# Two-layer conditioned attention, second layer: shifted-score matmuls put singly between key and query matmuls

## The reference

```
xn = layer_norm(x, norm_w, norm_b)
q = (xn @ q_w + q_b).reshape(Bx, Tx, H, -1)
k = (xn @ k_w + k_b).reshape(Bx, Tx, H, -1)
att = softmax(einsum('bnhl,bmhl->bnmh', q, k) + (1.0 - mask) * -1000000.0, axis=2)
v = ((xn @ v_w + v_b) * src_mask[:, :, None]).reshape(Bx, Tx, H, -1)
y = einsum('bnmh,bmhl->bnhl', att, v).reshape(Bx, Tx, Dx)
h = layer_norm(y, sb_norm_w, sb_norm_b) * (1.0 + scale) + shift
return x + silu(h) @ out_w + out_b
```

## Time and profile before

| what | value |
|---|---|
| median of 3 runs | 2480.9 us (2477.12 to 2482.09) |
| profiled execution | 2484.31 us, its span 2482.5 us |
| TensorE matmul records | 2359.0 us, 95% of the span |
| TensorE weight loads | 2125.6 us, 86% |
| VectorE, ScalarE, GpSimd | 63%, 33%, 24% |
| mean granted TensorE clock | 0.967 of full speed |
| layer 2, one body without disturbance | 41.2 us |

### The profile page before, as it was taken

How to read it: one execution, slowest core, us unless ns; L and a number is a source line. 1 busy time by engine, 2 the same in 40 slices (tenths; PEclk the granted TensorE clock), 3 DMA queues, 4 the chain that set the end, 5 groups by cost and what they waited for, 6 DMA issues and landing times.

```text
span 2482.5 us, 43830 instructions
## 1 busy us (share of the span) xinstructions
PE 2359.0 (95%) x15670; PEld 2125.6 (86%) x15670; DVE 1557.4 (63%) x3441; ACT 823.2 (33%) x1893; POOL 601.7 (24%) x847
## 2 busy tenths in 40 slices
PE   7999999999999999968999999999999999999998
PEld 5888888888888888857989898998889898989897
DVE  4677777777777777654465655556565656555654
ACT  2233333333333333332333333333323333333332
POOL 0333333333333333232121212122221212121210
PEclk9999999999999999978999989999989999989997
DMA  6100000000000010014444434353524343433432
GB/s 238 72 34 35 36 35 34 34 34 34 34 34 34 34 35 34 25 47 95 105 96 111 94 91 114 86 120 86 120 73 115 90 117 89 117 83 100 105 93 54
DMA packets 90933, 187.14 MB, mean 75 GB/s; under 512 B 18708, under 2 KB 29394, under 8 KB 90904
## 3 DMA queue, kind: packets, MB, share of 16 engines
q1 hardware_dynamic: 88856, 186.23, 28.3%
q10 hardware_dynamic: 2048, 0.53, 0.1%
HBM read 51.81 MB, written 33.69 MB: 34 GB/s over the span
## 4 chain that ended last, share of the span: by engine, by line
PE 47%; DVE 5%; issue 2%; POOL 1%; DMA 0%; ACT 0%; DVEq 0%; POOLq 0%; SPq 0%
PE bank L1423 7%; PE bank L439 5%; PE bank L441 5%; PE bank L440 5%; PE bank L430 5%; PE bank L431 5%; PE bank L1413 4%; PE bank L432 4%; PE bank L1439 4%; DVE h_lo L1207 2%; DVE z L1176 1%; DVE stats_y L1181 1%; POOL ve_y L1073 1%; POOL rstd_y L1075 1%; PE bank L1372 1%
## 5 line engine op out<-in xcount | busy, mean ns | idle before, releaser
L439 PE MATMUL bank<-xT_hi,w_hi 128*128 128x256 f32 x1536 | 446.4, 291 | 2.6 <-DVE xT_lo L1145 1.4
L440 PE MATMUL bank<-xT_lo,w_hi 128*128 128x256 f32 x1536 | 448.1, 292 | 0.0
L441 PE MATMUL bank<-xT_hi,w_lo 128*128 128x256 f32 x1536 | 445.0, 290 | 0.0
L1154 DVE SCALAR_TENSOR_TENSOR parts<-bank,qk_bias,parts 128x256 fp32r<-128x256 f32 x256 | 112.1, 479 | 432.9 <-ACT parts L1284 432.9
L1423 PEld LDWEIGHTS bank<-v,prob 128*128 128x128 f32 x2048 | 317.6, 195 | 12.7
L430 PE MATMUL bank<-w_hi,xT_hi 128*128 128x512 f32 x768 | 317.0, 413 | 0.0
L432 PE MATMUL bank<-w_lo,xT_hi 128*128 128x512 f32 x768 | 314.6, 410 | 0.0
L431 PE MATMUL bank<-w_hi,xT_lo 128*128 128x512 f32 x768 | 314.4, 409 | 0.0
L439 PEld LDWEIGHTS bank<-xT_hi,w_hi 128*128 128x128 f32 x1536 | 293.2, 191 | 4.8 <-DVE xT_lo L1145 1.8
L440 PEld LDWEIGHTS bank<-xT_lo,w_hi 128*128 128x128 f32 x1536 | 293.3, 191 | 1.9
L1423 PE MATMUL bank<-v,prob 128*128 128x33 f32 x2048 | 293.3, 251 | 0.0
(11 more groups left out here) (163 smaller groups left out, 4232.9 us busy)
## 6 DMA issues: line engine op xcount, KB each, us to landing
stack<-parts SPq DMA_DIRECT2D x768, 128.0 KB
xr<-in_x SPq DMA_DIRECT2D x32, 512.0 KB, 3.5
x_between_layers<-x SPq DMA_DIRECT2D x64, 256.0 KB, 2.0
xr<-x_between_layers SPq DMA_DIRECT2D x32, 512.0 KB, 3.6
out<-y_out SPq DMA_DIRECT2D x64, 256.0 KB, 2.0
w_emb<-in_L_cond_W_emb SPq DMA_DIRECT2D x4, 1024.0 KB, 9.9
w_emb<-in_L_cond_emb_w SPq DMA_DIRECT2D x4, 1024.0 KB, 4.8
raw<-in_L_cond_Wq SPq DMA_DIRECT2D x1, 1024.0 KB, 5.5
```

Of the source, the lines that this page charges most:

```text
L439: yield nc.tensor.matmul(dst, w_hi[:, m, c, fs], a_hi[:, c], start=(first and c == 0), stop=False)
L440: yield nc.tensor.matmul(dst, w_hi[:, m, c, fs], a_lo[:, c], start=False, stop=False)
L441: yield nc.tensor.matmul(dst, w_lo[:, m, c, fs], a_hi[:, c], start=False, stop=(c == C - 1))
L1154: nc.vector.scalar_tensor_tensor(parts[:, LO[n], c].rearrange("p b t -> p (b t)"), ps[QK_BANKS[n][c // 2]][:, at:at + PAIR * P], qk_bias[: ...
```

## The change

`weight_scores` becomes a generator that gives a step after every matmul. In the bodies with a previous pair, its 16 matmuls for the first sequence are put singly behind the first 16 of the 24 matmuls of key blocks 2 and 3, and those for the second sequence behind the first 16 of the 24 of query blocks 0 and 1. Behind the loop the two runs of 16 stay as they are. The transpose of the maxima keeps its place behind the 16th key matmul, and the two waits on `top` keep theirs ahead of key blocks 0 and 2.

```diff
--- before.py
+++ after.py
@@ -1412,7 +1412,9 @@
                 for a in range(HC):
                     last = nc.tensor.matmul(ps[W_BANKS[j]][:, a * P:(a + 1) * P], stack[0:K_SHIFTED, 1, a, j, b, :],
                                             stack[0:K_SHIFTED, 0, a, j, b, :], start=True, stop=True)
-                last.then_inc(s["w_ps"], 1)
+                    if a == HC - 1:
+                        last.then_inc(s["w_ps"], 1)
+                    yield
 
         def mixed(prev, b):
 
@@ -1453,18 +1455,19 @@
 
         def body(i, first, more, last):
             pe.wait_ge(s["xT_lo"], seq(PAIR, i, PAIR))
-            for f in range(C):
-                if not first and f % 2 == 0:
-
-                    pe.wait_ge(s["top"], seq(PAIR * C, i - 1, C + f // 2 + 1))
-                keys = projected(i, 1, (f,))
-                if not first and f == 1:
-                    run(islice(keys, 4))
-                    shift_row(i - 1, 1)
-                run(keys)
-                if not first and f % 2:
-                    weight_scores(i - 1, f // 2)
-            run(projected(i, 0, (0, 1)))
+            if not first:
+
+                pe.wait_ge(s["top"], seq(PAIR * C, i - 1, C + 1))
+            keys = projected(i, 1, (0, 1))
+            run(islice(keys, 16))
+            if not first:
+                shift_row(i - 1, 1)
+            run(keys)
+            if not first:
+
+                pe.wait_ge(s["top"], seq(PAIR * C, i - 1, C + 2))
+            woven(projected(i, 1, (2, 3)), () if first else weight_scores(i - 1, 0))
+            woven(projected(i, 0, (0, 1)), () if first else weight_scores(i - 1, 1))
             if first:
                 run(projected(i, 0, (2, 3)))
             else:
@@ -1497,7 +1500,7 @@
         bodies(pe, NP, body)
         shift_row(NP - 1, 1)
         for b in range(PAIR):
-            weight_scores(NP - 1, b)
+            run(weight_scores(NP - 1, b))
         for b in range(PAIR):
             run(mixed(NP - 1, b))
         for b in range(PAIR):
```

## The result

The changed kernel takes 2486.0 us (median of 10 runs, 2483.3 to 2490.8); the kernel before, run beside it, 2478.2 us (10 runs, 2475.1 to 2486.4). The ratio is 1.0031, its 95% interval 1.0019 to 1.0043: 7.8 us slower, and clear of no change. The forecast was 2472.5 us, faster. The executions that were profiled lie above these medians: 2484.31 us for the kernel before, and for the changed kernel the slowest of its ten.

A forecast was written before the change was run, and what follows sets the result against it. TensorE was taken as the bound, its matmul records covering 95% of the span. From the profiled 2484.3 us, 3.7 direct and 4.7 clock gave 2475.9, or 2472.5 on the median; range 2456 to 2487.

The forecast's parts named there:

- What a score costs between long matmuls: Step pricing a single shifted score among key or query matmuls: 0.108 us, against 0.112 in a burst.
- fixed part: Constant of about −0.004 us per group of short matmuls, fitted as 0.1122 n − 0.004 for a group of n.
- stated ends: Limits for a single score's price: 0.102 us (9.9 us less in all) and 0.1195 us (7.4 us more).
- direct term: TensorE time saved on 992 woven scores: (0.112 − 0.108) × 992 = 3.7 us less, 0.12 us a body.
- single transpose: Transpose of the maxima, one short matmul among keys, priced at 0.10 us and taken as the low end.
- "switching" rival: Each woven score costs a full key's 0.1195 us: 7.4 us more plus a clock fall, 2488.3 to 2494.6; chance 0.14.
- The clock term: TensorE's granted clock falling to 1.2 GHz in five loop bodies, just after pair-end waits; each fall costs 4.7 to 6.3 us.
- one fall fewer: Chosen as likeliest: four clock falls in the loop instead of five, 4.7 us less.
- The two waits: TensorE's pair-end waits for normalised rows (31.6 us) and the gated rows' low part (34.0 us), claimed to keep their length.
- The exponentials, the shift rows and the copies: Work around the weaves claimed to cost nothing; copies into the stack start 1.9 us later, with 3.8 us of slack left.
- Loads are not hidden: Denies the rival that streams cover weight loads in the weaves: 0.053 us a score, 58 us less, 2422; chance 0.08.

The follow-up runs named there:

- by-twos kernel: The changed kernel with the weave in groups of two: two keys or queries, then two scores; 2479.3 us, ratio 1.0001 to the kernel before.
- key_added: The kernel before with one more 256-column matmul ahead of the keys in each body with a previous pair; 2494.4 us, ratio 1.0061.
- key_less: The kernel before without one matmul of the second layer's keys, for timing only; 2469.9 us, ratio 0.9957.
- after_key_less: The changed kernel without one matmul of the second layer's keys, for timing only; 2473.9 us, ratio 0.9977 to the kernel before.
- filled pair: The kernel before and the changed kernel, each with three 512-column throwaway matmuls in each of TensorE's two pair-end waits; 2452.4 and 2452.3 us.
- before_mixed_first: The kernel before with all mixing matmuls of the second sequence ahead of the value rows; 2460.1 us, ratio 0.9922.
- before_spread: The kernel before with the second sequence's mixing matmuls two behind each of the first eight value matmuls, transposes of z after them; 2423.8 us, ratio 0.977.

## Why the prediction was wrong

**What a score costs between long matmuls.** This is the step that failed. The prediction fitted a fixed part of −0.004 us per group through groups of 16 and of 2 and read 0.108 us off for a group of one. Measured: 0.1138, within the stated ends but on the other side of the burst's 0.112. The direct term is +0.9 us by the body's length instead of −3.7. (0.0018 × 992 would be 1.8, but the whole stretch with the keys behind the weave is only 0.001 us a score longer.) The fit had two points with a difference of 0.002 us, and the single transpose that seemed to confirm it has a load of 16 columns, where a score has 128. The by-twos kernel is cheaper than both bursts and singles, so the price does not go on falling from two to one. Why a single costs more than a pair, no run shows.

The "switching" rival set its threshold at 0.2315 us for a key and a score. At 0.2333 it holds in kind, with a quarter of its price inside the weave and an eighth by the body (0.9 us instead of 7.4).

**The clock term.** It was set at one fall fewer, as a choice: −4.7 us. The changed kernel lost 6.9 us more to the clock instead, one fall more in its profile. The runs show that this goes with the sign of the length: longer bodies had more time at 1.2 GHz, shorter ones less, in key_added, key_less and after_key_less. Had the body become 0.12 us shorter, the forecast would have stood: key_less, with just that body, took 2469.9. The prediction knew that a fall costs more than the direct term, but took the number of falls as free of it; so a wrong sign of 0.15 us a body (41.12 forecast, 41.27 measured) became a miss of 13.5 us. A small direct loss with one fall more, 2480.9 + 0.9 + 6.3 = 2488.1, had no chance of its own; nearest was the "switching" rival with 0.14, which had the larger direct loss. That 2486.0 lies inside the stated range is luck: its upper end was put together from a direct gain and the edge of that rival.

**What held.** The two waits kept their length. The exponentials, the shift rows and the copies cost nothing, with the copies 2.0 us later for the 1.9 forecast. Loads are not hidden more deeply: a pair is at 0.233, not 0.173.
The Trainium skill (TensorE: Matmul & The Clock Gate, LDWEIGHTS) gives 128/1.2 = 107 ns for a load of 128 columns, and what the prediction drew from it held: at 0.1138 us a single score costs no less than such a load. The page's figure does not tell singles from twos or bursts.

**What stays open.** What the 0.03 us of the body are made of: with half the scores woven the body is already 41.27 us long. And how many falls a given length brings, and why. Between 41.24 and 41.27 us the median rose by 7 us beyond the work; between 41.21 and 41.24 it did not move by more than its interval. That the length acts by where in time the waits come is the prediction's reading; no run tests it apart from the length. Single runs of one kernel spread by over 10 us, as by one or two falls. The filled pair settles that the difference goes with the falls, not the function that makes it 7 us.

## What to carry to other kernels

A matmul of 128 columns or fewer with a weight load of 128 cost 0.110 to 0.114 us here wherever it stood, near the price of the load; weaving it between longer ones moved its price by 2% either way. Price the clock before the matmuls: here two waits of 1 us in a body of 41 cost 32 us in falls beside their own 60, and the way to get them back was to start the chain behind them earlier, with short matmuls kept apart. When two orders differ by tenths of a per cent, compare the granted clock of all their runs, not two profiles, or compare them with the falls removed, by fillers in the waits.

## What the runs showed of the hardware

The clock fell without any idle time as well: at the end of a run of 42 instructions with 33 columns, TensorE's records covering every microsecond, it went to 1.2 GHz in every body (136.5 us in the loop of before_mixed_first). With the same instructions in groups of four between 512-column matmuls, behind a run of 14, it stayed at 1.00 (before_spread). Useless matmuls in the waits made the kernel faster, 2452.4 for 2478.9 us. And a change of 0.14 us in a body of 41.2 moved the time by 15.6 us, 11 of them beyond the work; the granted clock of its runs puts 12 us on the clock.
